# Layer 1's four wide chunks in two parts, two subtractions a tile on VectorE with products in PSUM, operands in two PSUM banks

## The reference

```python
h = x0
for i in range(3):
    Wk = Ws[i].reshape(128, h.shape[1], 32)
    xk = relu(einsum('bhd,bmd,ohm->bod', h, x0, Wk) + bs[i][None, :, None])
    if i != 2:
        outs.append(xk[:, :64]); h = xk[:, 64:]
    else:
        outs.append(xk)
return concatenate([o.sum(axis=-1) for o in outs], axis=1)
```

## Time and profile before

| | |
|---|---|
| timed runs | 1838.84 us median (1838.52 to 1838.84) |
| profiled execution | 1838.24 us, its span 1836.4 us, mean granted clock 0.997 |
| PE busy | 1799.4 us, 98% |
| DVE busy | 1555.1 us, 85% |
| POOL busy | 1464.3 us, 80% |
| ACT busy | 1096.3 us, 60% |
| DMA | 112 GB/s on average |

### The profile page before, as it was taken

The page is one execution under the profiler, slowest core; times in us unless marked ns, Lnnn a source line. Parts: engine busy times, 40 slices in busy tenths (PEclk is TensorE's granted clock), DMA queues, the critical chain, the costliest instruction groups (busy, mean ns, idle before and its releaser), DMA issues.

```text
span 1836.4 us, 17679 instructions
## 1 busy us (share of the span) xinstructions
PE 1799.4 (98%) x6284; PEld 1184.2 (64%) x6284; DVE 1555.1 (85%) x851; ACT 1096.3 (60%) x899; POOL 1464.3 (80%) x323
## 2 busy tenths in 40 slices
PE   4899999999999999999999999999999999999998
PEld 2566666666666666666666666666666666666665
DVE  5989888888888888898888888888888988888886
ACT  3665666656566656656666565666566566665663
POOL 2787887877877878878878778778788788787785
PEclk9999999999999999999999999999999999999999
DMA  6333323323323333333233233233332332332310
GB/s 230 130 96 119 129 85 129 130 80 128 130 84 129 114 101 129 95 121 129 85 129 131 80 128 121 93 129 114 101 129 87 129 129 85 129 131 79 129 33 20
DMA packets 56455, 205.78 MB, mean 112 GB/s; under 512 B 12721, under 2 KB 14001, under 8 KB 47921
## 3 DMA queue, kind: packets, MB, share of 16 engines
q1 hardware_dynamic: 55408, 204.00, 33.3%
q10 hardware_dynamic: 960, 0.66, 0.1%
HBM read 153.75 MB, written 0.52 MB: 84 GB/s over the span
## 4 chain that ended last, share of the span: by engine, by line
PE 93%; issue 1%; DVE 1%; ACT 1%; POOL 0%; POOLq 0%; SPq 0%; DMA 0%; ACTq 0%
PE ACC L440 23%; PE ACC L456 19%; PE ACC L453 19%; PE ACC L450 19%; PE ACC L431 11%; PE ACC L434 3%; DVE ZS L257 1%; POOL ZL L339 0%; ACT ZH L361 0%; POOLq L71 0%; DVE ZW L252 0%; ACT HP L354 0%; DMA H<-H 0%; SPq L168 0%; DVE S L278 0%
## 5 line engine op out<-in xcount | busy, mean ns | idle before, releaser
L339 POOL TENSOR_TENSOR ZL<-ZS,ZH 128x2048 fp32r<-128x2048 f32 x319 | 1464.1, 4617 | 366.5 <-ACT ZH L361 366.5
L361 ACT ACTIVATE ZH<-ZS 128x2048 fp32r<-128x2048 f32 x384 | 734.6, 1913 | 599.7 <-PE ACC L456 415.3
L257 DVE TENSOR_TENSOR ZS<-HP,X 128x2048 f32<-128x2048 f32 x384 | 870.7, 2281 | 149.0 <-ACT HP L354 149.0
L450 PE MATMUL ACC<-ZH,WL 128*128 128x512 f32 x1536 | 498.3, 446 | 8.0 <-ACT ZH L361 8.0
L440 PE MATMUL ACC<-ZW,WF 128*128 128x512 f32 x1024 | 460.2, 592 | 0.0
L456 PE MATMUL ACC<-ZL,WH 128*128 128x512 f32 x1536 | 421.5, 396 | 8.2 <-POOL ZL L339 8.0
L453 PE MATMUL ACC<-ZH,WH 128*128 128x512 f32 x1536 | 421.6, 396 | 0.0
L450 PEld LDWEIGHTS ACC<-ZH,WL 128*128 128x128 f32 x1536 | 289.9, 189 | 153.3 <-issue 99.6
L252 DVE TENSOR_TENSOR ZW<-HP,X 128x2048 f32<-128x2048 f32 x128 | 292.3, 2283 | 101.2 <-PE ACC L440 101.2
L456 PEld LDWEIGHTS ACC<-ZL,WH 128*128 128x128 f32 x1536 | 287.6, 188 | 81.4 <-POOL ZL L339 11.5
L453 PEld LDWEIGHTS ACC<-ZH,WH 128*128 128x128 f32 x1536 | 289.4, 188 | 70.6
(11 more groups left out here) (32 smaller groups left out, 165.5 us busy)
## 6 DMA issues: line engine op xcount, KB each, us to landing
X<-in_xrows SPq DMA_DIRECT2D x62, 2048.0 KB, 7.6
H<-H SPq DMA_DIRECT2D x512, 64.0 KB, 2.0
XD<-in_xdup SPq DMA_DIRECT2D x64, 256.0 KB, 3.0
H<-H SPq DMA_DIRECT2D x128, 128.0 KB, 2.3
X<-in_xrows SPq DMA_DIRECT2D x4, 1024.0 KB, 9.8
X<-in_w SPq DMA_DIRECT2D x6, 256.0 KB, 13.1
WF<-in_w SPq DMA_DIRECT2D x2, 256.0 KB, 12.8
out<-XD SPq DMA_DIRECT2D x3, 128.0 KB, 1.8
```

The costliest lines, as they stand in the source:

```text
L257: nc.vector.tensor_tensor(ZS[:, n % SSLOTS, :, :], h, x, ALU.mult).then_inc(prod_ready, 1)
L339: nc.gpsimd.tensor_tensor(ZL[:, n % SSLOTS, :, :], ZS[:, n % SSLOTS, :, :], ZH[:, n % SSLOTS, :, :], ALU.subtract).then_inc(low_by_pool, 1)
L361: nc.scalar.activation(ZH[:, n % SSLOTS, :, :], ZS[:, n % SSLOTS, :, :], ACT.Copy).then_inc(high_ready, 1)
L450: nc.tensor.matmul(ACC[layer][:, :], wl[:, g, :], ZH[:, n % SSLOTS, g, :], start=(k == 0 and g == 0), stop=False)
```

## The change

Layer 1's group becomes a split group from tile 2 on (`HEADS` = 2; tiles 0 and 1 stay plain), so that 28 of 33 chunks are in two parts. Its weights are split at the start (`W1H`, `W1L`); the fifth chunk's weights are a tensor of their own, `W5`. A table, `kind`, says who subtracts: POOL for layer 1 and for q1 and q3, DVE ("vector") for q0 of layers 2 and 3. For these two groups DVE writes the product into PSUM (`ZP`, four banks), ACT rounds it from there, and DVE subtracts from there. ZS is now a ring of four slots for POOL's groups and the plain ones; `ZH` has four slots, `ZL` three, with releases of their own. To make room in PSUM, the accumulators are a ring of two banks, and the operands of all layers are a ring of two banks, `HP0` and `HP1`, filled by five copies of 128 x 512 a tile; a copy waits until the products of the use two before have been made (`wait_use`). `XD` has one buffer instead of two. W1 and W1T are loaded by SP, into X's third slot, ahead of the second half of X. A spread of hidden rows is four DMAs instead of five.

```diff
+def kind(i, layer, q):
+
+    if layer == 0:
+        return "plain" if i < HEADS else "pool"
+    return ("vector", "pool", "plain", "pool")[q]
...
-        ACC = [ps(f"ACC{n}", [128, T]) for n in range(3)]
-        XDP = ps("XDP", [128, T])
-        HP = [ps("HP2", [128, 2, T]), ps("HP3", [128, 2, T])]
+        ACC = [ps(f"ACC{n}", [128, T]) for n in range(BANKS)]
+        HP = [ps(f"HP{n}", [128, T]) for n in range(BANKS)]
+        ZP = ps("ZP", [128, G, T])
...
+            def load_xd(t):
+                if t >= 1:
+                    sp.wait_ge(operand_copied, USE_NO[t - 1, 0, 0] + 1)
+                sp.dma_start(XD[:, :], xdup[t, :, :]).then_inc(xd_loaded, 16)
...
             load_xd(0)
             load_x_half(0, 0)
+            sp.dma_start(W1, w1[:, 0:G, :]).then_inc(w1_loaded, 16)
+            sp.dma_start(W1T, w1t).then_inc(w1_loaded, 16)
+            sp.dma_start(W5[:, :], w1[:, G, :]).then_inc(w5_loaded, 16)
             load_x_half(0, 1)
...
-                    if t == XSLOTS - 1:
+                    if t == 2:
+                        sp.wait_ge(w1_low, 1)
+                        sp.wait_ge(plain_used, HEADS)
+                    if t == 3:
                         sp.wait_ge(w_low, 2)
...
+                if kind(*g) == "vector":
+                    if VECTOR_NO[g] >= 1:
+                        dve.wait_ge(low_by_dve, VECTOR_NO[g])
+                    nc.vector.tensor_tensor(ZP[:, :, :], h, x, ALU.mult).then_inc(vector_ready, 1)
+                    return
+                m = SLOT_NO[g]
+                if m >= PSLOTS:
+                    before = SLOTTED[m - PSLOTS]
+                    if kind(*before) == "plain":
+                        dve.wait_ge(plain_used, PLAIN_NO[before] + 1)
+                    else:
+                        dve.wait_ge(low_by_pool, POOL_NO[before] + 1)
+                done = plain_ready if kind(*g) == "plain" else pool_ready
+                nc.vector.tensor_tensor(ZS[:, m % PSLOTS, :, :], h, x, ALU.mult).then_inc(done, 1)
...
+            def low(i, layer, q):
+                n = SPLIT_NO[i, layer, q]
+                if n >= LSLOTS:
+                    dve.wait_ge(low_used, n - LSLOTS + 1)
+                dve.wait_ge(high_ready, n + 1)
+                nc.vector.tensor_tensor(ZL[:, n % LSLOTS, :, :], ZP[:, :, :], ZH[:, n % HSLOTS, :, :],
+                                        ALU.subtract).then_inc(low_by_dve, 1)
...
+            def wait_use(u):
+
+                i, layer, lay = USES[u]
+                if layer == 0:
+                    act.wait_ge(narrow_ready, i + 1)
+                else:
+                    act.wait_ge(pool_ready, POOL_NO[i, layer, 2 * lay + 1] + 1)
...
-            def copy_hidden(t, layer):
-                act.wait_ge(h_loaded[layer], 16 * (1 + NB) * (t + 1))
-                if t >= 1:
-                    act.wait_ge(prod_ready, split_before(t + layer, layer + 1, NS - 1) + 1)
-                nc.scalar.activation(HP[layer][:, :, :], H[layer][:, :, :], ACT.Copy).then_inc(h_copied[layer], 1)
+            def copy_operand(i, layer, lay):
+                u, t = USE_NO[i, layer, lay], i - layer
...
+                if u >= BANKS:
+                    wait_use(u - BANKS)
+                nc.scalar.activation(HP[u % BANKS][:, :], src, ACT.Copy).then_inc(operand_copied, 1)
...
+                if kind(*g) == "plain":
+                    plain(g, acc, W1, True)
+                    narrow(i, acc, True)
+                else:
+                    split_high(g, acc, W1H, W1L, True)
+                    narrow(i, acc, False)
+                    split_low(g, acc, W1H, True)
```

More of the change, by code:

```diff
@@ L14 @@
 XC = M // NB
-C1 = 5
 ROWS = 128 + XC
@@ L239, in layer1, with narrow @@
+            def narrow(i):
+                u = USE_NO[i, 0, 0]
                 if i < HEADS:
@@ L297, in _ @@
                 if live(i):
-                    layer1(i)
+                    product(i, 0, 0)
+                    if i == 0:
+                        sum_w1()
+                    narrow(i)
+                if i == 1:
+                    low_w1()
                 if i == 2:
@@ L422, in _, with wait_bank, plain @@
         def _(pe):
+            def wait_bank(i, layer):
+                n = LAYER_NO[i, layer]
+                if n >= BANKS:
+                    wait_relu(pe, *LAYERS[n - BANKS])
+                return ACC[n % BANKS][:, :]
+            def plain(g, acc, w, first):
+                pe.wait_ge(plain_ready, PLAIN_NO[g] + 1)
+                m = SLOT_NO[g]
+                for c in range(G):
+                    last = nc.tensor.matmul(acc, w[:, c, :], ZS[:, m % PSLOTS, c, :], start=(first and c == 0), stop=False)
+                last.then_inc(plain_used, 1)
@@ new lines, in split_high, with split_low @@
+            def split_high(g, acc, wh, wl, first):
+                n = SPLIT_NO[g]
+                pe.wait_ge(high_ready, n + 1)
+                for c in range(G):
+                    nc.tensor.matmul(acc, wl[:, c, :], ZH[:, n % HSLOTS, c, :], start=(first and c == 0), stop=False)
+                for c in range(G):
+                    last = nc.tensor.matmul(acc, wh[:, c, :], ZH[:, n % HSLOTS, c, :], start=False, stop=False)
+                last.then_inc(high_used, 1)
+            def split_low(g, acc, wh, end):
+                n = SPLIT_NO[g]
+                wait_low(pe, g)
+                for c in range(G):
+                    last = nc.tensor.matmul(acc, wh[:, c, :], ZL[:, n % LSLOTS, c, :],
+                                            start=False, stop=(end and c == G - 1))
+                last.then_inc(low_used, 1)
@@ L423, in layer1, with narrow @@
+            def narrow(i, acc, end):
+                pe.wait_ge(narrow_ready, i + 1)
+                nc.tensor.matmul(acc, W5[:, :], ZN[:, :], start=False, stop=end).then_inc(narrow_used, 1)
             def layer1(i):
+                g, acc = (i, 0, 0), wait_bank(i, 0)
                 if i == 0:
                     pe.wait_ge(w1_summed, 1)
-                else:
-                    pe.wait_ge(relu_done[0], i)
-                n = wide_before(i, 0)
-                pe.wait_ge(wide_ready, n + 1)
@@ L430, in layer1 @@
-                for g in range(G):
-                    last = nc.tensor.matmul(ACC[0][:, :], W1[:, g, :], ZW[:, n % WSLOTS, g, :], start=(g == 0), stop=False)
-                last.then_inc(wide_used, 1)
-                pe.wait_ge(narrow_ready, i + 1)
-                nc.tensor.matmul(ACC[0][:, :], W1[:, G, :], ZN[:, :], start=False, stop=True).then_inc(narrow_used, 1)
-            def plain(i, layer):
-                n = wide_before(i, layer)
-                pe.wait_ge(wide_ready, n + 1)
-                for g in range(G):
-                    last = nc.tensor.matmul(ACC[layer][:, :], WF[:, layer - 1, g, :], ZW[:, n % WSLOTS, g, :],
-                                            start=False, stop=False)
-                last.then_inc(wide_used, 1)
@@ L444, in split @@
-            def split(i, layer, q):
-                k = SPLIT.index(q)
-                n = split_before(i, layer, k)
-                wh, wl = WH[:, layer - 1, k, :, :], WL[:, layer - 1, k, :, :]
-                pe.wait_ge(high_ready, n + 1)
-                for g in range(G):
-                    nc.tensor.matmul(ACC[layer][:, :], wl[:, g, :], ZH[:, n % SSLOTS, g, :],
-                                     start=(k == 0 and g == 0), stop=False)
-                for g in range(G):
-                    nc.tensor.matmul(ACC[layer][:, :], wh[:, g, :], ZH[:, n % SSLOTS, g, :], start=False, stop=False)
-                wait_lows(pe, n + 1)
-                for g in range(G):
-                    last = nc.tensor.matmul(ACC[layer][:, :], wh[:, g, :], ZL[:, n % SSLOTS, g, :],
-                                            start=False, stop=(k == NS - 1 and g == G - 1))
-                last.then_inc(split_used, 1)
+                    pe.wait_ge(w5_loaded, 16)
@@ L490, in _ @@
                             turn12(BLOCKS - 1)
-                        if q == PLAIN:
-                            plain(i, layer)
-                        else:
-                            split(i, layer, q)
+                        group(i, layer, q, acc)
             pe.wait_ge(sums3, TILES)
```

307 lines of the change are left out of this document (160 added, 147 removed).

## The result

The changed kernel takes 1797.07 us (median of four, 1795.95 to 1797.59) against 1838.84 before: 41.8 us less, ratio 0.9772 (95% interval 0.9758 to 0.9786). The forecast was 1797.

The account below looks back on a forecast made before the run. PE (TensorE) was taken as the bound: 1838.2 us profiled, less 39.1 for layer 1 and 2.5 at the start, gives 1796.6, predicted as 1797. Its own range was 1792 to 1803; to hold eight in ten, 1790 to 1812.

Parts of the forecast that it names:

- PE's saving: Layer 1 on PE, split from tile 2: 2.80 us instead of 3.43, 0.63 less a tile, 39.1 over 62 tiles.
- DVE's slack: Per tile DVE needs 26.2 us against PE's 27.32, 1.1 spare; rival that DVE becomes the bound, 1801 to 1828: 12%.
- The prediction's 0.26: Estimated loss in us a tile on four touched DVE instructions, if a PSUM source costs 120 fixed cycles against 58.
- The rings: Buffer slots reused in mid span: the longest way round still reaches PE in time, 1.8 us left at the tightest.
- The way round to layer 1's subtraction: From DVE's product for layer 2's plain group through ACT to POOL, ending at 30.5; PE wants it at 32.85.
- The operand ring: Two operand banks, five copies a tile; rival: two copies each idle DVE 2.25 us, time 2008 us, chance 5%.
- Start and end: Outside mid span: start between 4.3 us won and 4 lost, 2.5 won taken; end taken as 0.
- the bound of 4.3: Most us that could be won at PE's first matmul, from DVE's old 4.31 wait for W1T.
- The 4 that might be lost at tile 2: Start: tile 2's layer 1 needs a rounding and a subtraction, 1.91 + 4.62, less 2.73 that PE spends meanwhile.
- 2.59 for POOL: PE's wait for POOL at the end of the old kernel; the last layer 3 was to keep it, gain 0.
- ACT out of PSUM: Two of seven ACT roundings read PSUM: 0.1 us more each, at worst 0.3 a tile, hidden by over 7 slack.

## Why the prediction was right

*PE's saving.* 62 x 0.63 = 39.1 forecast, 62 x 0.634 = 39.3 measured; the run with layer 1 plain shows that it is layer 1 and nothing else.

*DVE's slack.* The decisive guess was that an instruction between PSUM and SBUF costs what a product costs, wherever the PSUM end is: 2.20 taken, 2.19 to 2.20 from start to start measured, and a wait of 1.26 a tile where 1.2 was forecast. The run with 2048 elements more turns DVE into the bound at the round that the sum gives, the one with 1024 makes it the bound by 0.09, and the run with the products in SBUF shows what stood behind the choice of place: 36 us. By the Trainium skill's rule on PSUM sources ("VectorE: DVE Perf Modes", The TRN2 errata) the subtraction would have become dearer. These runs don't show that: it took 2280, 76 ns less than the old median and as good as the 2276 that one with two SBUF inputs took at the least. The prediction's 0.26 by that rule was also twice too high, since only the two subtractions have a new PSUM source; the products had theirs before.

*The rings.* The way round to layer 1's subtraction had 1.8 us to spare by my listing. In the trace POOL's second subtraction of a row of three begun at 1001.24 (13.75 in all) ends at 1010.4, and PE takes it at 1012.43 (from the chain): 2.0.

```profile
1001.24 13.75 POOL L356 TENSOR_TENSOR ZL<-ZS,ZH 128x2048 fp32r<-128x2048 f32 x3 [1.44 <-ACT ZH L398]
```

```profile
1012.43 0.92 PE ACC L499 x4
```

The operand ring costs nothing: DVE waited for a copy five times in the whole run, two of them before 42 us and two after 1764, in the last tiles, and once for 1.6 us between.

*Start and end.* 2.5 us taken for the start and 0 for the end; the traces have 2.2 and 0.8. That the start came out so near is luck, for neither term behind it was right. PE's first matmul came 5.4 us earlier, beyond the bound of 4.3. The 4 that might be lost at tile 2 were two waits, 1.91 for ACT's rounding and the rest for POOL's subtraction; the 4.13 that are there are the wait for the rounding alone, and the number agrees by chance. The slower clock behind PE's waits stood in no term: the rows gave it in slices of 46 us and tenths, in which a fall of 3.4 us doesn't show. Nor did the end keep its chain: instead of 2.59 for POOL, PE waits 3.15 for ACT.

*ACT out of PSUM.* Taken 0.1 us too dear, without effect.

What the prediction did not see, because its rows held it as a given, is that the 0.93 of a pass hangs on where its operand starts.

## What to carry to other kernels

Add up each engine's work per round, and compare it with the bound's new round, not with the old one; then list for every ring which use frees which slot, each use and not only the one that waits today. Where VectorE and GpSimd work side by side, keep one of VectorE's two inputs in PSUM. Before comparing two kernels by a per cent, look whether their buffers start at other addresses: 32 bytes were worth half of this change.

## What had not been expected of the hardware

A pass of four fp32r matmuls, 128x512, took 0.917, 0.931, 0.933 or 0.94 us, by the start of its moving operand (the one that streams through PE, here ZH or ZL) modulo 128 bytes (64, 0, 32, 96), at the same granted clock (1.00, the 2.4 GHz level, in mid span). Plain fp32 groups kept 3.43 us at each placement tried (64, 0 and 32).
